# A macaron transformer on one core: the first batch's last stage moved into the second batch's attention, and a new chain table, whole shares, an unsplit bias and gates in place in the expert loop

## The reference

```
x = x + 0.5 * MoE(layernorm(x))          # 16 experts, top 4, 128 -> 2x128 -> 128, router bias
x = x + SSM(layernorm(x))                # scan over the tokens, gelu, product, layernorm
x = x + 0.5 * MoE(layernorm(x))          # the same weights again
x = x + 0.5 * LoRA_MoE(layernorm(x))     # base product + 8 rank-16 experts, 2 null ones, top 2
x = x + Attention(layernorm(x))          # 16 heads of 8, a decay with the distance
x = x + 0.5 * LoRA_MoE(layernorm(x))     # the same weights again
MoE:  act = (clip(up) + 1) * gate * sigmoid(1.702 * gate), gate = min(., 7)
      out = sum over experts of share * (act @ down + down_bias)
```

## Time and profile before

| | us |
|---|---|
| median of 3 runs | 791.61 (789.17 to 791.88) |
| the profiled execution | 787.95 |
| its span, from the first to the last instruction | 786.1 |
| PE busy | 679.1 (86%) |
| ACT busy | 557.4 (71%) |
| DVE busy | 482.3 (61%) |
| POOL busy | 271.2 (34%) |

### The profile page before, as it was taken

How to read it: one execution, slowest core, us unless ns; L and a number is a source line. 1 busy time by engine, 2 the same in 40 slices (tenths; PEclk the granted TensorE clock), 3 DMA queues, 4 the chain that set the end, 5 groups by cost and what they waited for, 6 DMA issues and landing times.

```text
span 786.1 us, 11233 instructions
## 1 busy us (share of the span) xinstructions
PE 679.1 (86%) x3617; PEld 399.5 (51%) x3617; DVE 482.3 (61%) x1258; ACT 557.4 (71%) x789; POOL 271.2 (34%) x298
## 2 busy tenths in 40 slices
PE   3789788878889899999777769999999999999587
PEld 2566566656566667777555532332323223232364
DVE  4789877878798778988856552344322223222474
ACT  4657574666767666655453569999999999999243
POOL 3286456665667556455620430112000000000110
PEclk9999999999999999999958689999999999999858
DMA  9002232323223223333200189100199100000001
GB/s 261 11 1 70 80 97 80 90 84 91 86 82 97 90 84 115 102 124 114 73 15 0 27 179 194 31 1 1 20 187 196 29 1 1 1 1 1 3 1 54
DMA packets 31343, 54.55 MB, mean 69 GB/s; under 512 B 4624, under 2 KB 13280, under 8 KB 29776
## 3 DMA queue, kind: packets, MB, share of 16 engines
q1 hardware_dynamic: 30128, 53.38, 26.3%
q0 software_dynamic: 224, 0.34, 0.2%
q10 hardware_dynamic: 928, 0.06, 0.1%
HBM read 35.71 MB, written 1.28 MB: 47 GB/s over the span
## 4 chain that ended last, share of the span: by engine, by line
PE 33%; ACT 31%; issue 14%; DVE 13%; POOL 7%; ACTq 0%; DVEq 0%; POOLq 0%
ACT raw_w L836 26%; PE bank L1421 7%; PE bank L1423 6%; PE bank L1422 6%; POOL act_parts L576 4%; PE bank L1546 2%; PE bank L1543 2%; PE bank L1544 2%; PE bank L1461 2%; DVE act L1094 2%; DVE bank L1083 1%; POOL rstd L523 1%; DVE up L1072 1%; ACT xt L665 1%; PE bank L1476 1%
## 5 line engine op out<-in xcount | busy, mean ns | idle before, releaser
L836 ACT ACTIVATE raw_w<-bank,minus_c 128x1024 f32<-128x1024 f32 x256 | 259.6, 1165 | 1.8 <-PE bank L1722 0.7
L576 POOL TENSOR_TENSOR act_parts<-act,act_parts 128x512 fp32r<-128x512 f32 x128 | 167.4, 1309 | 120.6 <-ACT act_parts L737 99.9
L1266 DVE TENSOR_TENSOR bank<-bank,fix 128x256 f32<-128x256 f32 x128 | 55.3, 433 | 177.9 <-PE bank L1699 177.9
L723 ACT ACTIVATE bank<-bank,b_gate 128x512 f32<-128x512 f32 x112 | 74.1, 662 | 113.9 <-PE bank L1423 64.4
L1421 PE MATMUL bank<-xn_parts,w_hi 128*128 128x512 f32 x256 | 109.6, 428 | 20.1 <-ACT bank L723 10.2
L1072 DVE TENSOR_SCALAR up<-bank,b_up 128x512 f32<-128x512 f32 x128 | 95.5, 746 | 36.0 <-PE bank L1423 32.3
L1423 PE MATMUL bank<-xn_parts,w_hi 128*128 128x512 f32 x256 | 102.7, 401 | 0.0
L1422 PE MATMUL bank<-xn_parts,w_lo 128*128 128x512 f32 x256 | 102.4, 400 | 0.0
L520 POOL TENSOR_SCALAR var_eps<-mean_var 128x4 f32<-128x4 f32 x28 | 7.4, 263 | 236.2 <-DVE mean_var L940 234.9
L1094 DVE SCALAR_TENSOR_TENSOR act<-up,bank 128x512 f32<-128x512 f32 x128 | 86.6, 676 | 0.0
L737 ACT ACTIVATE act_parts<-act 128x512 fp32r<-128x512 f32 x128 | 79.8, 623 | 4.2 <-DVE act L1094 4.2
(11 more groups left out here) (204 smaller groups left out, 1057.6 us busy)
## 6 DMA issues: line engine op xcount, KB each, us to landing
grow<-scores SPq DMA_DIRECT2D x68, 256.0 KB, 3.2
early<-scores SPq DMA_DIRECT2D x44, 256.0 KB, 3.2
raw_w<-in_gate_up SPq DMA_DIRECT2D x4, 512.0 KB, 8.8
w_lo<-gelu_parts SPq DMA_DIRECT2D x8, 256.0 KB, 5.1
w_lo<-act_parts SPq DMA_DIRECT2D x8, 256.0 KB, 5.5
w_hi<-gelu_parts SPq DMA_DIRECT2D x6, 256.0 KB, 4.7
w_hi<-act_parts SPq DMA_DIRECT2D x6, 256.0 KB, 5.5
x_tok<-in_x SPq DMA_DIRECT2D x4, 256.0 KB, 4.4
```

The lines of the kernel that those rows point to most:

```text
L576: pool.tensor_tensor(act_lo[:, j % NACT, :], act[:, j % NACT, :], act_hi[:, j % NACT, :].bitcast(F32), ALU.subtract).then_inc(s["lo_ready" ...
L723: eng.activation(out, bank[:, G, :], ACT.Gelu_apprx_sigmoid, bias=b_gate[:, e:e + 1]).then_inc(s["glu_ready"], 1)
L836: eng.activation(probs[:, u % NP, :], pair, ACT.Exp, bias=minus_c[:, b:b + 1])\
```

## The change

1. Chunks 0 and 1 (the first batch) take their last stage in the second batch's attention. The table EARLY says after which step TensorE, and after which unit VectorE and ScalarE, issue which of its operations. All of its groups on TensorE use bank 7, so each waits until the one before has been read (early_free). The work that ScalarE does for these chunks in the old tail (rounding copies, layernorm rows, copies from PSUM) is done by VectorE, but for the router's exp. In the second batch all blocks of the attention are summed in bank 6 and turned into bank 7; take_out, turn and normalize come 2, 2 and 4 units or steps earlier, and the first weighing of a block waits for the copy of the block before. The tail runs on chunks 2 and 3 alone.
2. The expert loop: new BASE, STEPS and SINGLE; the gate and up halves of job 0 are issued in EARLY_SLOT, before its shares; add_out stands ahead of expert_weighted.
3. Whole shares: in chunks 1 to 7 of the 8 of the loop the router writes the share once, unsplit, and it is transposed to rows 0 to 15 or 32 to 47 and copied once. The bias of the down half is there one float32 product with the unsplit bias (a third copy of it is loaded), in place of two split ones.
4. Gates in place: after the first 16 jobs the gate half goes to bank 0, 2 or 3 in turn, and the gelu, the weighting and its reading work in that bank. The gate product waits for expert_act of three jobs before; the gelu waits for its product alone.

```diff
-BASE = {"in": (-14, -10, 2, 9), "ssm": (20, 34, 50, 66)}
+BASE = {"in": (-13, -12, 0, 11), "ssm": (20, 35, 51, 67)}
 STEPS = {
-    "pe": {"in": {"take_in": 0, "t2": 4, "logits": 6, "scores": 10},
+    "pe": {"in": {"take_in": 0, "t2": 5, "logits": 6, "scores": 10},
            "ssm": {"t1": 0, "t2": 4, "proj": 10, "inner_t1": 11, "inner_t2": 15, "b_t1": 20, "b_t2": 24, "logits": 30, "scores": 36}},
     "act": {"in": {"take_in": 0, "rows": 3, "hi": 5, "exp": 8, "out": 12},
            "ssm": {"rows": 3, "copy": 5, "gelu": 8, "inner_rows": 14, "scale": 16, "b_rows": 23, "hi": 25, "exp": 32, "out": 37}},
-    "dve": {"in": {"stats": 0, "lo": 5, "pick": 6, "drop": 6, "total": 9, "share": 9},
+    "dve": {"in": {"stats": 0, "lo": 5, "pick": 6, "drop": 6, "total": 8, "share": 9},
            "ssm": {"stats": 0, "scan_in": 5, "scan": 6, "resid": 10, "inner_stats": 11, "b_stats": 20, "lo": 25, "pick": 30, "drop": 30, "total": 32, "share": 35}},
-    "pool": {"in": {"norm": 1},
+    "pool": {"in": {"norm": 0},
            "ssm": {"norm": 0, "y": 7, "gelu_lo": 9, "inner_norm": 12, "add": 16, "b_norm": 21}},
...
 SINGLE = {
     "pe": {"mix0": 106, "mix1": 109, "mix2": 112},
-    "act": {"split_small": -9, "split0": -6, "split1": -3, "split2": 0, "split3": 1, "split_squares": 11, "mix0": 107, "mix1": 110, "mix2": 113},
-    "dve": {"split_small": -9, "split0": -6, "split1": -2, "powers": 8, "mix2": 114},
-    "pool": {"split2_0": 1, "split2_1": 2, "split2_2": 4, "split3_0": 5, "split3_1": 6, "split3_2": 8, "split_squares0": 12, "split_squares1": 13},
+    "act": {"split_small": -9, "split0": -7, "split1": -3, "split2": 0, "split3": 2, "split_squares": 11, "mix0": 107, "mix1": 110, "mix2": 113},
+    "dve": {"split_small": -9, "split0": -6, "split1": -2, "powers": 13, "mix2": 114},
+    "pool": {"split2_0": -2, "split2_1": 2, "split2_2": 4, "split3_0": 8, "split3_1": 6, "split3_2": 8, "split_squares0": 12, "split_squares1": 13},
 }
 FIRST_SLOT = min(BASE["in"])
+EARLY_SLOT = BASE["in"][0] + STEPS["pe"]["in"]["scores"]
 LOOP_NORMS = [(BASE["in"][c], LN_FFN0A, c) for c in range(NC)] + \
...
+EARLY = {
+    "pe": {69: ("heads", 0), 71: ("heads", 1), 73: ("out", 0), 77: ("out", 1), 79: ("t1", 0), 85: ("t2", 0), 87: ("t1", 1),
+           93: ("logits", 0), 95: ("t2", 1), 97: ("logits", 1), 101: ("scores", 0), 103: ("z", 0), 105: ("weights", 0),
+           109: ("scores", 1), 111: ("z", 1), 113: ("back", 0), 117: ("weights", 1), 119: ("turn", 0), 121: ("back", 1),
+           125: ("turn", 1)},
+    "dve": {141: ("heads_hi", 0), 142: ("heads_lo", 0), 144: ("heads_hi", 1), 145: ("heads_lo", 1), 148: ("attn_add", 0),
+            156: ("attn_add", 1), 161: ("stats", 0), 166: ("rows", 0), 173: ("hi", 0), 174: ("lo", 0), 176: ("stats", 1),
+            180: ("rows", 1), 188: ("pick", 0), 189: ("drop", 0), 193: ("hi", 1), 194: ("lo", 1), 195: ("total", 0),
+            197: ("pick", 1), 198: ("drop", 1), 199: ("share", 0), 203: ("total", 1), 205: ("score_copy", 0),
+            207: ("share", 1), 208: ("z_copy", 0), 212: ("zs", 0), 213: ("zs_hi", 0), 216: ("zs_lo", 0),
+            220: ("score_copy", 1), 225: ("z_copy", 1), 229: ("add", 0), 237: ("zs", 1), 238: ("zs_hi", 1),
+            239: ("zs_lo", 1), 240: ("out_copy", 0), 244: ("add", 1), 252: ("out_copy", 1)},
+    "act": {190: ("exp", 0), 201: ("exp", 1)},
+}
...
+def whole_shares(r, c):
+    return 1 <= r * NC + c < 2 * NC
+def score_rows(r, c):
+    return 2 * E0 * ((r * NC + c) % 2)
+def gate_bank(j):
+    return 0 if spread_by_pe(j) else (0, 2, 3)[j % 3]
+def weighted_bank(j):
+    return (2, 3)[j % 2] if spread_by_pe(j) else gate_bank(j)
...
+        EARLY_BANK = 7
+        def early_chunk(last_stage, c):
+            return last_stage and c < QC
+        def stage_bank(usual, r, c):
+            return EARLY_BANK if early_chunk(r == 3, c) else usual
...
+        def o_bank(n):
+            return 6 + n % 2 if n < G4 * QC else 6
+        def turned_bank(n):
+            return o_bank(n) if n < G4 * QC else EARLY_BANK
+        turn_after = {KB // 2 * G4 * QC * 2 + KB * i + 3: ("turned", G4 * QC + i - 1) for i in range(G4 * QC)}
+        early_uses = [use for _, use in sorted(list(EARLY["pe"].items()) + list(turn_after.items()))]
...
                 eng.wait_ge(s["score_psum_ready"], kr + 1)
-                if r < 2 and kr >= 1:
-                    if kr >= 2:
-                        eng.wait_ge(s["scores_stored"], 16 * (kr - 1))
-                    eng.activation(score_f, bank[nr:nr + E0, scores_bank(r), :], ACT.Copy)\
-                       .then_inc(s["score_f_ready"], 1)
-                eng.activation(score_t[0:nr, chunk(c)], bank[0:nr, scores_bank(r), :], ACT.Copy)\
-                   .then_inc(s["score_ready"], 1)
+                if whole_shares(r, c):
+                    at = score_rows(r, c)
+                    if kr >= 3:
+                        eng.wait_ge(s["scores_stored"], 16 * (kr - 2))
+                        eng.wait_ge(s["down_done"], E0 * (kr - 2) + 1)
+                    eng.activation(score_f(r, c), bank[at:at + E0, scores_bank(r, c), :], ACT.Copy).then_inc(s["score_ready"], 1)
+                else:
+                    eng.activation(score_t[0:nr, chunk(c)], bank[0:nr, scores_bank(r, c), :], ACT.Copy)\
+                       .then_inc(s["score_ready"], 1)
             def expert_glu(j):
                 e = j % E0
...
                 else:
-                    eng.wait_ge(s["act_ready"], j - 1)
-                    out = bank[:, S[j % 2], :]
-                eng.activation(out, bank[:, G, :], ACT.Gelu_apprx_sigmoid,
+                    out = bank[:, gate_bank(j), :]
+                eng.activation(out, bank[:, gate_bank(j), :], ACT.Gelu_apprx_sigmoid,
                                bias=b_gate[:, e:e + 1]).then_inc(s["glu_ready"], 1)
                 if up_on_act(j):
...
+                    if u in EARLY["act"]:
+                        router_exp(3, EARLY["act"][u][1])
...
+                whole = whole_shares(r, c)
+                for dst in (share[:, b, :, 0:ne],) + (() if whole else (share_hl[:, b, :, 0:ne].bitcast(F32R),)):
                     ins = eng.scalar_tensor_tensor(out=dst, in0=picked[:, b, :, 0:ne],
                                                    scalar=0.5 if moe else 1.0,
                                                    in1=recip[:, b, :, None].to_broadcast([128, TPC, ne]),
                                                    op0=ALU.mult, op1=ALU.mult)
+                if whole:
+                    ins.then_inc(s["share_ready"], 1)
+                    return
+                step = kr + 1 - (min(kr, 2 * NC - 1) if kr >= 1 else 0)
                 ins.then_inc(s["share_step"], 1)
-                eng.wait_ge(s["share_step"], kr + 1)
+                eng.wait_ge(s["share_step"], step)
                 eng.tensor_tensor(share_hl[:, b, :, ne:2 * ne].bitcast(F32R), share[:, b, :, 0:ne],
                                   share_hl[:, b, :, 0:ne], ALU.subtract).then_inc(s["share_ready"], 1)
...
                     n = u // (2 * KB)
-                    if u % (2 * KB) == 5 and n > 0:
+                    if u % (2 * KB) == (5 if u < UNITS else 3) and n > 0:
                         take_out(n - 1)
-                    if u % (2 * KB) == 13 and n > 0:
+                    if u % (2 * KB) == (13 if u < UNITS else 9) and n > 0:
                         normalize(n - 1)
+                    if u in EARLY["dve"]:
+                        early_step(*EARLY["dve"][u])
                 take_out(NB * G4 * QC - 1)
-                head_lo(0)
+                head_lo(QC)
                 normalize(NB * G4 * QC - 1)
-                for c in range(1, NC):
-                    head_lo(c)
+                head_lo(QC + 1)
...
+                if slot > E0 and slot % E0 == 2:
+                    add_out(slot // E0 - 1)
                 if 0 <= slot < JOBS:
                     expert_weighted(slot)
-                if slot > E0 and slot % E0 == 2:
-                    add_out(slot // E0 - 1)
                 side("dve", slot, chains, single)
...
-                if j >= 1:
+                if j >= 1 and j <= E0:
                     pe.wait_ge(s["glu_ready"], j)
-                split_matmul(bank[:, G, :], w0_hi[:, e, 0, :], w0_lo[:, e, 0, :],
+                if j >= E0:
+                    pe.wait_ge(s["act_ready"], j - 1 if j < E0 + 2 else j - 2)
+                split_matmul(bank[:, gate_bank(j), :], w0_hi[:, e, 0, :], w0_lo[:, e, 0, :],
                              xn_hi[:, at], xn_lo[:, at], True, True).then_inc(s["g_ready"], 1)
                 if j >= 1:
...
-                    pe.matmul(out, db_hi[:], score_t[:, chunk(c)], start=True, stop=False)
-                    pe.matmul(out, db_lo[:], score_t[:, chunk(c)], start=False, stop=False)
+                    if whole_shares(j // E0 // NC, c):
+                        at = score_rows(j // E0 // NC, c)
```

(43 more changed lines are left out.)

230 lines of the change are left out of this document (158 added, 72 removed).

## The result

The changed kernel takes 770.83 us (median; 769.22 to 772.11), against 791.71 (789.17 to 791.88) for the kernel before: a ratio of 0.974, 95% interval 0.971 to 0.977. The profiled execution took 770.2, its span is 768.4, the mean granted clock 0.946. The forecast was 777, range 766 to 790.

What follows compares the result with a forecast made beforehand. TensorE, with stalls from other engines, bounds the loop; ScalarE the attention; no engine the tail. -15 + 12.8 - 7.4 - 3.9 - 1.0 + 3.1 - 3.5 = -14.9 us: profiled 787.95 becomes 773, median 777, range 766 to 790.

Steps and rivals of the forecast that it cites:

- the case that I held likeliest: Whole kernel: the sum of all terms as it stands, 777 us, own range 771 to 784, chance 0.50.
- Tail, -15: Tail: without chunks 0 and 1, 13.0 us less for the chunks and 1.9 less for output products; ends -10 and -19.
- the rule against part 1: Tail: activity lifts TensorE's clock, so a thinner tail stays at the lower level; six last products give 1.2 us back.
- Attention, +12.8: Second batch's attention: twenty inserted TensorE groups, bank waits, router exps and late fixes cost 12.8 us; bounds +4 and +19.
- free 0.17 us a step: Attention: TensorE has about 0.17 us free in each 2.00 us step, so two steps rebuild the 0.29 us of slack.
- length less 0.29: Attention: TensorE may be late by 0.29 us, so an inserted group costs ScalarE its length minus that.
- cheap insertions: Rival, attention: free TensorE time swallows the insertions for +4 us, giving 768; chance 0.16.
- Gates in place, -7.4: Expert loop: three gate banks save 5.1 us of gate waits and 2.3 of low-part waits; ends 0 and -17.9.
- the loop's stall only moves: Rival, expert loop: the single up bank catches what the gates gave up, the table brings nothing; 789, chance 0.14.
- Chain table and addition, -3.9: Expert loop: later transposes and an earlier addition save 3.9 of 4.6 us of waits; ends 0 and 6.5.
- Whole shares -1.0, unsplit bias +3.1: Expert loop: fewer router operations on VectorE save 1.0 us; seven full-precision bias products cost TensorE 3.1 more.
- Start, -3.5: Loop start: job 0's six products move into idle time ahead of the shares, saving 3.5 us; ends 0 and -3.85.

Runs made afterwards that it cites:

- run 12: Changed kernel with unread filler products in TensorE's tail waits, none ahead of the output products: 762.96 us, ratio 0.965 to the kernel before.
- the stage alone: Kernel before with only the last stage of chunks 0 and 1 moved into the second batch's attention, old loop kept: 782.20 us, ratio 0.988.
- run 10: Changed kernel with the six products of each back inside the attention issued three and three in neighbouring steps: 771.10 us, ratio 0.978 to the kernel before.
- run 9: Kernel before with the turns of its attention repeated or moved as probes of insertion price: 800.59 us beside 789.74; profiled once.
- run 3: Changed kernel with the old chain table and old table of single steps: 775.60 us, ratio 0.979 to the kernel before.
- run 4: Changed kernel with shares written three times and the bias as two split products again: 771.57 us, ratio 0.975 to the kernel before.
- the repetition: The changed kernel once more, unaltered, as neighbour for other runs: 769.16 us, ratio 0.972 to the kernel before.
- run 7: Changed kernel with job 0's gate and up halves issued in slot 0 again: 771.32 us, ratio 0.975 to the kernel before.
- the loop alone: Kernel before with only the expert loop's edits, attention and tail as before: 777.86 us, ratio 0.982.
- run 11: Changed kernel with unread filler products in TensorE's tail waits, ten of them ahead of the output products: 770.16 us, ratio 0.974 to the kernel before.

## Why the prediction was right, and where it was not

The sign and the size hold: 777 forecast, 770.8 measured, in the range, though 0.2 us below the 771 to 784 of the case that I held likeliest. By its own parts:

- **Tail, -15: right.** It is -14.6. What I had to choose, 13.0 between 8.5 and 17.0, came out as 9.9 up to the first addition and 4.9 between first and last, less 1.7 of output products (4.44 before; 2.72 now, from 732.47 to 735.19): 13.1. That it comes so near is luck: the choice was the middle of two bounds. "From the last exp to the end some 43 us": 43.4 from its end. The clock stays low to the end, as the rule against part 1 had it, and run 12 shows what that holds back: 5.4 us, not the 1.2 that I gave it for six products. I take it that this is because from 750 us on some 26 products follow one another nearly without a pause; which of them are on the path was not worked out.
- **Attention, +12.8: the step that failed.** It is +5.5 in the two profiles and +5.4 with the stage alone. The failed term is the "free 0.17 us a step". I took it from two score groups of 0.43 each. They were apart because TensorE waited for ScalarE between them; when it is behind, the two run side by side and a step takes 1.40 us (run 10), so 0.6 us are free in it. The price of a lone insertion, length less 0.29, was right within 0.01 for one, 0.08 for two and 0.11 for four turns in a row (run 9). But a second insertion two steps later finds more than 0.29 rebuilt: a turn is then free. So half of the transposes cost nothing, the backs 0.88 and 1.02 for 1.32. The twenty insertions cost 5.6 us where I had 9.6, and the turns of the blocks, which I had left at 2.3, only 1.1; the two router exps cost 0.24 for 0.6. The 2 us for the copy of the single bank are not there either: no wait of TensorE for VectorE. This was the rival "cheap insertions", at a chance of 0.16. Its +4 (4.5 by its own numbers, 15.4 less 10.9) is nearer than my 12.8, and so is its time of 768; its reason is a like one, with more free time than it counted.
- **Gates in place, -7.4: wrong.** The wait for ScalarE fell, from 10.2 to 3.3, but the sum of the waits within a job did not: 27.3 before, 26.1 after, and up to 382 us the kernel with one bank has 27.7 against 27.0. This part went the way of the rival "the loop's stall only moves". I had the next wait in the wrong place, too: those for the up half fell (9.4 to 5.6) where I wrote that they would grow, and those for GpSimd's low part doubled.
- **Chain table and addition, -3.9: too small.** Waits for the addition went from 4.6 + 1.9 to 0.5, the waits for shares in the loop from 3.0 to nothing, which I had not counted, and with the old tables 3 to 6 us come back (run 3), part of it at the first shares.
- **Whole shares -1.0, unsplit bias +3.1.** The product was sized right: 1.05 us against 0.66, so +2.7 in seven, between the ends of 0.2 and 5.0. But with split parts the kernel is not faster (run 4), so the router's and the copies' part is worth about what the bias costs. Which of them was not tried apart.
- **Start, -3.5: too large, as far as it can be told.** Job 1's gates come 1.9 earlier (0.7 in the profile of the repetition, 30.27); undone it costs about 2.2. The shares were pushed back by 3.3. I had named two causes as a risk, the six products and the earlier second chunk in VectorE's queue. With the new table only the second acts: VectorE starts the last step of the first shares at 25.12 us instead of 21.86, behind the router steps of the second chunk, and the six products move nothing (run 7). With the old table (run 3) that step starts at 21.84, and there the products are in the way: the transposes start at 23.65.
- **Loop as a whole.** Its terms summed to -12.7. The two profiles have -9.5, the loop alone -14.1 by its time. The sum is right within this spread, its parts are not: too much for the gates, too little for the order of the chains.

That the total is only 6.2 us off owes something to luck. Profile against profile I forecast -14.9, and the span fell by 17.7: the attention cost 7.3 less than forecast, but the loop gained 3.2 less, the tail 0.4 less, and the middle took 0.8 more. The other 3 us are in the median, which I carried over as 3.7 above the profiled execution and which is 0.6 above it now.

## What to carry to other kernels

Take the free time of an engine from a stretch in which it is behind, not from one in which it waits: lengths there hold hidden waiting, and groups that could run side by side are drawn out. Count waits by what they have in common: releasers within one job trade time among themselves when a buffer is added, while a wait that comes from the order of two chains is gone when the order is changed. And where a thin stage runs at the lower clock, look at what it costs from there to the end: products in waits that are long enough gave 5.4 us, the same products where the engine could not use them cost 4.1.

## What the runs showed of the hardware that I had not expected

The middle stage, the same code in all these kernels, takes 78.2 to 79.5 us in nine of fourteen profiles and 81.4 to 82.7 in five (that of before is one of the nine). All five have a stretch at the lower clock in the middle's last 16 us; of the nine only the one of run 4 has a short one. After, and the kernel with one gate bank, timelines of TensorE:

```profile
447.26 0.30 PE L1577 MATMUL bank<-sq_hi,xn_parts 128*128 128x128 f32 x1 [0.87 <-ACT raw_w L891]
447.40 0.28 PE L1578 MATMUL bank<-sq_hi,xn_parts 128*128 128x128 f32 x1
```

```profile
449.56 0.45 PE L1578 MATMUL bank<-sq_hi,xn_parts 128*128 128x128 f32 x1 [0.86 <-ACT raw_w L892]
449.81 0.41 PE L1579 MATMUL bank<-sq_hi,xn_parts 128*128 128x128 f32 x1
```

Behind the same waits (1.50 and 0.87 us; 1.53 and 0.86) the clock stays up in one and is at the lower level in the other, where the products of 128 columns start 0.21 to 0.25 apart instead of 0.11 to 0.14, until 455.7. What decides was not tried; it makes some 3 us between profiles of the same code, as much as several of the edits here.

TensorE also stands 2.7 to 3.2 us before the output products (in run 11 before the fillers ahead of them) with nothing that the profile shows to wait for, in every kernel here (the earlier trace rows have it before); no edit of these runs touched that.
